# Attention's first score tiles ahead of the kernel's branch, V projected in two parts

## The chip, the cores and the metric

One core of a Trainium2 chip runs the kernel. The metric is the device time of one execution in microseconds, the median of several runs. Lower is better.

## The reference, cut to what matters

```python
x = x + xattn(layernorm(x), ctx_768, ...)      # x: 1 x 1024 x 128, ctx_768: 1 x 6404 x 96
x = x + ffn(layernorm(x), ...)                 # a main path and 2 of 8 experts, hidden size 512
...
q = (query @ Wq + bq)                          # 16 heads of 8
k = (key_value @ Wk + bk)
v = (key_value @ Wv + bv)
attn = clip(q k^T * 8 ** -0.5, -10000, 10000)
attn = softmax(attn)                           # 16 x 1024 x 6404
x = attn @ v
...
return x @ Wo + bo
```

The reference replaces attention by a mean where a NaN turns up and clips the scores. The kernel computes a bound of the scores at run time; if it holds, neither can occur and the softmax needs no maximum. That is the `safe` flag and the branch on it.

## The kernel before

**Stages.** The context (6404 rows of 96 numbers) is loaded, transposed on TensorE in 13 chunks of 512 rows into `ctxT` and projected to K^T, chunk by chunk (`ctx_transpose`, L941; `project_k`, L953). ScalarE evacuates both (`evac_ctxT`, L360; `evac_k`, L365). Meanwhile the queries are normalised (L571 to L595, scaled at L585), transposed, projected (L983) and evacuated (L496 to q, L498 to its absolute values).

**K and q through DRAM.** The score products run as sums over 32 rows, four heads side by side, each number split into a rounded part and a rest. VectorE makes the parts (`split_q` L616 and L618, `split_k` L626 and L627). SyncE stores them to DRAM (L396, L331) and loads them back in the layout of the products: `load_q` (L354, four loads of 128 KB a group of heads, each with a leading broadcast of 2), `load_k` (L341). K goes in ten segments of 5 tiles of 128 rows (the last with 4 rows more). The parts of a segment lie in one of two buffers, so that splitting segment s waits until segment s - 2 is stored:

```python
if s >= 2:
    dve.wait_ge(kparts_stored[s % 2], 16 * PARTS * (s // 2))
```

Each engine runs its instructions in the order in which they are written, and a wait holds up all behind it. In SyncE's queue q's loads stand ahead of K's first store.

**V and the bound.** Behind the K projections TensorE makes the bias rows (L992 to L994), V's 13 chunks (`project_v`, L964, evacuated by ScalarE, L373) and, between them, the bound (L1008, L1012, L1013). VectorE makes the flag (L669). Three chunks ahead of V's end the engines read it; ScalarE loads its Exp table there (L508). All that follows is written within the branch.

**The attention loop.** Eight passes (four groups of four heads, two halves of 512 queries each) go over the 51 K tiles. A score of one head and one K tile is a chunk of 128 x 512; three chunks are a score tile, in one of two PSUM buffers `ps`. For each of 500 tiles, TensorE computes the scores two tiles ahead (`score_tile`, L1077), ScalarE takes the exponential of all 128 x 1536 at once (L516) into one of four `probs` buffers, and TensorE multiplies with V (`values_step`, L1141, one step for each K tile once its four chunks are there; V's tail of 4 rows at L1127). The sums of a pass gather in one of the two banks `po`. The other bank is spare: `D_PLAN` names 27 steps of four chunks whose exponentials VectorE computes instead (L766 to L805), with the pass, the K tile, the tiles behind which its four scores are made, the heads' order, and the tile behind which its values are used. `SPARE` is the list of jobs in the spare bank, done strictly in turn: a job waits until VectorE has taken the one before it. At a pass's end the sums are transposed (L1099) and normalised. SyncE loads K for the next group behind its last use.

**The end.** Output projection, second normalisation and the feed-forward layers follow (L1017 to L1256). `region_ctx`, where the context stood, takes two experts' weights; `region_ctxT` held `ctxT` and then `probs`.

**POOL's work at the start:** constants, a row of ones in `ctxT` (a memset of 1 x 6432, L446), 12 small loads, the ones in V (`v9`, L460), more memsets.

Of the kernel before, what the change touches and what calls it, by code (L numbers as in the profile page):

```python
# [21 lines left out]
P = 128  # L22
# [31 lines left out]
V_ORDER = [0, KCH // 2] + [c for c in range(1, VCH) if c != KCH // 2]  # L54
NPR = 4
BO_BANK = 3 + (KCH - 3) % 3
FLAG_AHEAD = 3
BOUND_AT = 4
# [76 lines left out]
for gap in EPI_GAPS:  # L135
# [7 lines left out]

SPARE = sorted([(t, "score", GH * d + k) for d, (_, _, at, _, _) in enumerate(D_PLAN) for k, t in enumerate(at)]
               + [(NORM_AT[p], "tokens", p) for p in range(NP - 1)])
# [9 lines left out]
def tile_of_segment(p, s):  # L155
    return max(c for c, (n, _) in enumerate(CHUNKS)
               if STEPS[n][0] == p and (STEPS[n][1] < FULL and STEPS[n][1] // SEG_T == s)) // CPT
# [22 lines left out]
def build(nc, x, ctx, wq, bq, wk, bk, wv, bv, wo, bo, alpha, w_gate, b_gate, w1m, b1m, w2m, b2m,  # L180
# [4 lines left out]
    with ExitStack() as stack:  # L185
# [27 lines left out]
        pre = region_ctx[:, 2 * TOPK * HID:2 * TOPK * HID + CB * BANK].rearrange("p (c n) -> p c n", c=CB)  # L213
# [4 lines left out]
        ctxT = region_ctxT[0:CK + 1, 0:NK]  # L218
        tailT = sb("tailT", [CK + 1, P])
# [56 lines left out]
        probs = region_ctxT[:, 0:NPR * CPT * BANK].rearrange("p (b n) -> p b n", b=NPR)  # L276
# [25 lines left out]
        bounds_ready, bound_psum, gcol_ready, grow_psum, flag_ready = (sem(n) for n in ("bounds_ready", "bound_psum", "gcol_ready", "grow_psum", "flag_ready"))  # L302
# [8 lines left out]
        rows_psum, attention_done = sem("rows_psum"), sem("attention_done")  # L311
# [56 lines left out]
        def evac_v(act, nth):  # L368

            c = V_ORDER[nth]  # L370
            n = min(4, FULL + 1 - 4 * c)
            act.wait_ge(v_psum, nth + 1)
            act.activation(v9[:, 4 * c:4 * c + n, :, 0:D], po[nth % 2][:, 0:n * P].rearrange("p (t h d) -> p t h d", h=H, d=D),  # L373
                           ACT.Copy).then_inc(v_done, 1)


        def load_expert(engine, e):

# [6 lines left out]
        def _(sp):  # L385
# [17 lines left out]
            with sp.If(safe != 0):  # L403
                for s in range(1, NSEG):
                    store_k(sp, s)
                    if s >= 2:
                        load_k(sp, 0, s - 1)
# [886 lines left out]
```

## Time and profile before

| | |
|---|---|
| median of 3 runs | 794.51 us (794.29 to 796.16) |
| the profiled execution | 795.02 us |
| its span, first to last instruction | 793.2 us |
| TensorE busy | 728.6 us (92%) |
| ScalarE busy | 724.9 us (91%), of them 678.4 us in 500 exponentials |
| VectorE busy | 548.1 us (69%) |
| DMA engines' mean rate | 37 GB/s |

The durations below come from the profiled execution, whose time is 1.8 us over its span. PE is TensorE, PEld its weight loads, DVE VectorE, ACT ScalarE, POOL GpSimd, SPq the queue of SyncE. A product of f32 is two MATMUL instructions with a weight load each. Consecutive instructions of an engine overlap, so that what one costs is the distance from start to start. "[0.85 <-PE ps L1077]" says that the engine stood idle 0.85 us and what released it.

### The profile page before, as it was taken

What the parts mean: (1) busy time and instruction counts of PE and PEld (TensorE: products, weight loads), DVE (VectorE), ACT (ScalarE), POOL (GpSimd) and SP (SyncE); (2) the same over time, 40 slices, a digit from 0 to 9 for tenths busy, and PEclk for the clock granted to TensorE, in tenths of its full rate; (3) what the DMA queues carried; (4) which work ended last, traced back from release to release, by engine and by line L of the source; (5) the groups of instructions that cost most, each with busy time, mean ns of one, the idle gap of its engine ahead of it and who ended that gap; (6) DMA issues with size and microseconds to landing.
All of it is one profiled execution on the core that took longest, in us unless ns stands there. A gap on an engine that the chain in (4) does not pass through costs nothing.

```text
span 793.2 us, 13140 instructions
## 1 busy us (share of the span) xinstructions
PE 728.6 (92%) x5406; PEld 215.9 (27%) x5406; DVE 548.1 (69%) x760; ACT 724.9 (91%) x587; POOL 20.6 (3%) x36
## 2 busy tenths in 40 slices
PE   4988889999999999999899999999999989999898
PEld 2642222222222222222222222222222222222457
DVE  5634298789878978898788897897689882140220
ACT  3769999999999999999999999999999999999451
POOL 8000000000000000000000000000000000000000
PEclk9989999999999999999999999999999999999999
DMA  5258210011110000111100000111100000000010
GB/s 190 106 153 285 69 46 1 18 34 35 51 34 1 1 1 1 34 51 34 37 15 1 1 1 19 34 34 50 34 1 2 1 1 1 1 1 1 4 54 27
DMA packets 15324, 29.05 MB, mean 37 GB/s; under 512 B 2438, under 2 KB 5884, under 8 KB 15260
## 3 DMA queue, kind: packets, MB, share of 16 engines
q1 hardware_dynamic: 13562, 26.86, 11.0%
q8 instruction: 45, 0.74, 0.4%
q10 hardware_dynamic: 1218, 0.64, 0.3%
q0 software_dynamic: 480, 0.66, 0.3%
q14 instruction: 19, 0.16, 0.1%
HBM read 20.02 MB, written 8.13 MB: 35 GB/s over the span
## 4 chain that ended last, share of the span: by engine, by line
PE 53%; ACT 23%; issue 18%; DVE 3%; DMA 1%; POOLq 0%; SPq 0%; POOL 0%; ACTq 0%
PE po L1141 27%; ACT region_ctxT L516 22%; PE ps L1077 15%; PE ps L1222 2%; PE po L1232 1%; PE po L964 1%; PE ps L953 1%; DMA region_ctx<-in_ctx 1%; PE po L1127 1%; PE ps L941 1%; DVE xn L585 1%; PE po L1056 1%; DMA region_ctx<-in_w1e 0%; PE ps L1232 0%; PE ps L1072 0%
## 5 line engine op out<-in xcount | busy, mean ns | idle before, releaser
L516 ACT ACTIVATE region_ctxT<-ps 128x1536 f32<-128x1536 f32 x500 | 678.4, 1543 | 7.8 <-PE ps L1077 7.5
L1141 PE MATMUL po<-region_ctxT,v 128*9 128x512 f32 x2984 | 391.6, 597 | 0.5 <-ACT region_ctxT L516 0.5
L1077 PE MATMUL ps<-qst,region_k 32*128 32x512 f32 x1492 | 253.7, 495 | 42.3 <-ACT region_ctxT L516 41.5
L1077 PEld LDWEIGHTS ps<-qst,region_k 32*128 32x128 f32 x1492 | 97.2, 182 | 416.8 <-ACT region_ctxT L516 397.3
L766 DVE TENSOR_SCALAR region_kT<-po 128x512 f32<-128x512 f32 x108 | 74.1, 686 | 85.2 <-PE po L1077 85.2
L769 DVE SCALAR_TENSOR_TENSOR region_kT<-region_kT,po 128x512 f32<-128x512 f32 x108 | 73.4, 680 | 0.3
L1141 PEld LDWEIGHTS po<-region_ctxT,v 128*9 128x9 f32 x2984 | 44.3, 88 | 92.9 <-issue 89.4
L805 DVE SCALAR_TENSOR_TENSOR dres<-region_kT,dres 128x1024 f32<-128x1024 f32 x54 | 66.1, 1225 | 1.7
L802 DVE SCALAR_TENSOR_TENSOR dres<-region_kT,dres 128x1024 f32<-128x1024 f32 x54 | 65.8, 1218 | 0.1
L794 DVE SCALAR_TENSOR_TENSOR dres<-region_kT 128x1024 f32<-128x1024 f32 x54 | 65.7, 1218 | 0.0
L796 DVE SCALAR_TENSOR_TENSOR region_kT<-region_kT 128x1024 f32<-128x1024 f32 x54 | 65.7, 1217 | 0.0
L799 DVE SCALAR_TENSOR_TENSOR dres<-dres,region_kT 128x1024 f32<-128x1024 f32 x54 | 65.6, 1214 | 0.0
L1077 PE MATMUL po<-qst,region_k 32*128 32x512 f32 x108 | 52.1, 483 | 0.0
L785 DVE TENSOR_SCALAR region_kT<-region_kT 128x1024 uint32<-128x1024 uint32 x54 | 36.9, 683 | 0.0
L1141 PE MATMUL po<-dres,vd 128*9 128x512 f32 x216 | 28.2, 595 | 0.0
L748 DVE COPY region_kT<-po 128x512 f32<-128x512 f32 x8 | 5.5, 686 | 32.0 <-PE po L1127 32.0
L473 POOL TENSOR_TENSOR rstd<-rstd,powers 128x4 f32<-128x4 f32 x2 | 2.1, 1026 | 727.6 <-DVE rstd L580 727.6
L1077 PEld LDWEIGHTS po<-qst,region_k 32*128 32x128 f32 x108 | 19.6, 181 | 0.5 <-DVE region_kT L769 0.4
L703 DVE TENSOR_SCALAR region_ctx<-po,b1T 128x512 f32<-128x512 f32 x4 | 3.0, 751 | 19.2 <-PE po L1056 19.2
L360 ACT ACTIVATE region_ctxT<-ps 96x512 f32<-96x512 f32 (+1 forms) x13 | 7.5, 576 | 9.2 <-PE ps L941 9.2
L626 DVE CAST kparts<-region_kT 128x640 fp32r<-128x640 f32 (+1 forms) x10 | 4.9, 493 | 15.5 <-DMA k_dram<-kparts 14.5
L941 PE MATMUL ps<-ident,region_ctx 128*96 128x128 f32 x50 | 8.8, 309 | 7.2 <-DMA region_ctx<-in_ctx 7.2
(195 smaller groups left out, 304.3 us busy)
## 6 DMA issues: line engine op xcount, KB each, us to landing
region_k<-k_dram SPq DMA_DIRECT2D x40, 320.0 KB, 3.3
k_dram<-kparts SPq DMA_DIRECT2D x18, 320.0 KB, 4.3
qst<-q_dram SPq DMA_DIRECT2D x16, 128.0 KB
region_ctx<-in_ctx SPq DMA_DIRECT2D x2, 624.0 KB, 9.3
q_dram<-region_k SPq DMA_DIRECT2D x2, 512.0 KB, 2.7
k_dram<-kparts SPq DMA_DIRECT2D x2, 322.0 KB, 5.3
region_ctx<-in_ctx SPq DMA_DIRECT2D x1, 576.0 KB, 7.4
xres<-in_x SPq DMA_DIRECT2D x1, 512.0 KB, 4.4
```

The costliest lines, as they stand in the source:

```text
L516: act.activation(probs[:, t % NPR, :], ps[t % NSB][:, :], ACT.Exp, scale=ESCALE).then_inc(exp_ready, 1)
L766: d_count(("u", c), v.tensor_scalar(du[:, i % 2, part], src, MAGIC, None, ALU.add))
L769: v.scalar_tensor_tensor(df[:, i % 2, part], du[:, i % 2, part], MAGIC, src, ALU.subtract, ALU.subtract).then_inc(spare_taken, 1)
L785: d_count(("e", i), v.tensor_scalar(u.bitcast(U32), u.bitcast(U32), 23, None, ALU.logical_shift_left))
L794: d_count(("q1", i), v.scalar_tensor_tensor(res, f, A1, f, ALU.add, ALU.mult))
L796: d_count(("q2", i), v.scalar_tensor_tensor(q, f, A2, f, ALU.add, ALU.mult))
L799: d_count(("p1", i), v.scalar_tensor_tensor(res, res, B1, u, ALU.add, ALU.mult))
L802: d_count(("p2", i), v.scalar_tensor_tensor(res, q, B2, res, ALU.add, ALU.mult))
L805: v.scalar_tensor_tensor(res, f, R0, res, ALU.subtract, ALU.mult).then_inc(d_ready, 1)
L941: last = tr(dst[:, at:at + P], ctx_sb[:, t, :], ident[:, :])
L1077: return mm(dst, kst[r, kt * P:(kt + 1) * P], qst[r, g, queries], start=True, stop=True)
L1141: last = mm(dst[QUAD * j:QUAD * j + V9, :], w, src, start=first, stop=last_one, skip_group_check=True)
```

## The change

- **Order at the start.** `Sqrt`'s table load goes to ScalarE's beginning; the root comes behind the first chunk. K chunks run one earlier against the context's chunks. GpSimd's row of ones and the ones in V wait for the scaled queries.
- **V's chunks 0 to 4** are projected behind K's chunks 7 to 11 and taken by VectorE (`take_v`, L646 of the changed kernel) instead of ScalarE. Chunks 5 to 12 become spare jobs at tiles 5, 8, ... 26 of the first pass. So do the bound (tiles 3 and 6), its sum (9) and the bias rows (12).
- **Splits.** VectorE splits K's segments 0 to 3 behind its range reductions of chunks 2, 4, 7 and 9, segments 4 to 9 behind the spare jobs.
- **Ahead of the branch** stand now the Exp table load, the first 14 tiles, all K stores, the first group's K loads and all q loads.
- **Buffers.** `probs` move from `region_ctxT`, where ctxT is still read, to an own buffer and `region_ctx`; the absolute values of q are made by VectorE from q, and the bound's scale with them.
- **`D_PLAN`** keeps 27 steps, the first at tile 37 instead of 26, three instead of two in the last pass.

```diff
+NPRE = 14
+VPRE = 5
+V_AT = {c: 3 * c - 10 for c in range(VPRE, VCH)}
+BOUND_TILES, GSUM_TILE, ROWS_TILE = (3, 6), 9, 12
...
-    (0, 49, (26, 28, 31, 33), (3, 1, 2, 0), 48),
+    (0, 49, (37, 39, 42, 44), (0, 2, 3, 1), 56),
...
+    (7, 47, (479, 481, 485, 488), (3, 1, 0, 2), 499),
...
+SPLIT_BEHIND = {SPARE.index((V_AT[c], "v", c)): s for c, s in zip(range(VPRE, VCH), range(4, NSEG))}
...
+        probs_own = sb("probs_own", [P, CPT * BANK])
...
+            return probs_own[:, :] if n == 0 else region_ctx[:, (n - 1) * CPT * BANK:n * CPT * BANK]
...
             load_q(sp, 0)
-            store_k(sp, 0)
-            load_k(sp, 0, 0)
+            for s in range(NSEG):
+                store_k(sp, s)
+                if s != 1:
+                    load_k(sp, 0, max(s - 1, 0))
+            load_k(sp, 0, NSEG - 1)
+            load_k_tail(sp)
+            for g in range(1, NG):
+                load_q(sp, g)
             sp.wait_ge(flag_ready, 1)
...
+            pool.wait_ge(xn_ready, QT)
+            pool.memset(region_ctxT[CK:CK + 1, :], 1.0).then_inc(pads_ready, 1)
+            pool.wait_ge(pads_ready, 3)
+            pool.memset(v9[:, :, :, D:V9], 1.0).then_inc(vones_ready, 1)
...
+            act.activation(scratch[:, :], ones[0:1, 0:1], ACT.Exp).then_inc(table_step, 1)
...
+            exponentials(range(NPRE))
+            act.wait_ge(flag_ready, 1)
+            safe = act.value_load(flag[0:1, 0:1], min_val=0, max_val=1)
+            with act.If(safe != 0):
+
+                exponentials(range(NPRE, NT))
...
             for c in range(KCH - 1):
-                if c == 1:
+                if c == 3:
                     split_q()
+                    link(v.scalar_tensor_tensor(q_abs, qT[:, :], -1.0, qT[:, :], ALU.mult, ALU.max))
                 range_k(c)
-                if c == 4:
-                    split_k(0, link)
+                if c in (2, 4, 7, 9):
+                    split_k((2, 4, 7, 9).index(c), link)
+                if c >= KCH - 1 - VPRE:
+                    dve.wait_ge(v_psum, c - (KCH - 1 - VPRE) + 1)
+                    take_v(c - (KCH - 1 - VPRE), po[(c - (KCH - 1 - VPRE)) % 2]).then_inc(v_done, 1)
...
+                n = c - (KCH - 1 - VPRE)
+                if 0 <= n < VPRE:
+                    if n == 0:
+                        pe.wait_ge(q_ready, NHALF)
+                    if n >= 2:
+                        pe.wait_ge(v_done, n - 1)
+                    project_v(n, po[n % 2]).then_inc(v_psum, 1)
...
+                if kind == "v":
+                    last = project_v(i, po[1])
...
+            score_tile(0)
+            pe.wait_ge(k_ready, KCH)
+            score_tile(1)
...
+            score_tiles(range(NPRE))
+            pe.wait_ge(flag_ready, 1)
+            safe = pe.value_load(flag[0:1, 0:1], min_val=0, max_val=1)
+            with pe.If(safe != 0):
+                score_tiles(range(NPRE, NT))
```

The order of instructions, first on TensorE about the end of the K projections and the first scores. Before (L941 transposes, L953 K, L964 V, L1077 scores):

```order
L953 MATMUL ps<-region_ctxT,wk_sb 128x512 [waits k_ready,ctxT_ready] x2
L953 MATMUL ps<-region_ctxT,wk_sb 128x260 [waits k_ready,ctxT_ready]
L992 MATMUL ps<-bsum,ones 128x128 [waits k_ready,ffn_in]
L993 MATMUL ps<-mix,ones 128x1
L994 MATMUL ps<-ident,b1rows 128x36
L964 MATMUL po<-wv_sb,region_ctxT 128x128 [waits q_abs_ready,pads_ready,wv_in]
L964 MATMUL po<-wv_sb,region_ctxT 128x128 x7
L964 MATMUL po<-wv_sb,region_ctxT 128x128 [waits v_done]
```

Now (L983 transposes, L995 K, L1006 V, L1101 scores):

```order
L1006 MATMUL po<-wv_sb,region_ctxT 128x128 [waits v_done]
L1006 MATMUL po<-wv_sb,region_ctxT 128x128 x3
L983 MATMUL ps<-ident,region_ctx 96x128 [waits ctx_in4,ctxT_ready]
L983 MATMUL ps<-ident,region_ctx 96x128 [waits ctx_in4] x3
L995 MATMUL ps<-region_ctxT,wk_sb 128x512 [waits k_ready,ctxT_ready]
L1006 MATMUL po<-wv_sb,region_ctxT 128x128 [waits v_done]
L1006 MATMUL po<-wv_sb,region_ctxT 128x128 x3
L983 MATMUL ps<-ident,region_ctx 96x128 [waits ctx_in4,ctxT_ready]
L983 MATMUL ps<-ident,region_ctx 96x128 [waits ctx_in4]
L987 MATMUL ps<-ident,ctx_tail 96x4 [waits tail_in]
L995 MATMUL ps<-region_ctxT,wk_sb 128x512 [waits k_ready,ctxT_ready]
L1006 MATMUL po<-wv_sb,region_ctxT 128x128 [waits v_done]
```

V chunks whose place in PSUM is awaited (v_done) now stand ahead of the last K chunks, and the first scores stand right behind K.

On VectorE over the same stretch. Before (L611 range of K, L640 the tail of ctxT), nothing waits for a store between the first split and the last range:

```order
L626 CAST kparts<-region_kT 128x640
L627 TENSOR_TENSOR kparts<-region_kT,kparts 128x640 [waits dve_step]
L611 TENSOR_REDUCE kmax<-region_kT 128x1 [waits k_ready] x7
L640 COPY tailT<-region_ctxT 97x4 [waits pads_ready,ctxT_ready]
L640 COPY tailT<-region_ctxT 97x4 x3
L611 TENSOR_REDUCE kmax<-region_kT 128x1 [waits k_ready]
```

Now (L625 range of K, L640 and L641 the split, L646 V's evacuation):

```order
L625 TENSOR_REDUCE kmax<-region_kT 128x1 [waits k_ready] x3
L640 CAST kparts<-region_kT 128x640 [waits kparts_stored0]
L641 TENSOR_TENSOR kparts<-region_kT,kparts 128x640 [waits dve_step]
L646 COPY v<-po 128x64x8 [waits v_psum]
L625 TENSOR_REDUCE kmax<-region_kT 128x1 [waits k_ready]
L646 COPY v<-po 128x64x8 [waits v_psum]
L625 TENSOR_REDUCE kmax<-region_kT 128x1 [waits k_ready]
L640 CAST kparts<-region_kT 128x640 [waits kparts_stored1]
L641 TENSOR_TENSOR kparts<-region_kT,kparts 128x640 [waits dve_step]
L646 COPY v<-po 128x64x8 [waits v_psum]
```

Splits of segments 2 and 3, which wait for stores, stand ahead of V's evacuations.

At the end of TensorE's loop, now (L1186 and L1172 are `values_step`, L1223 the last pass's sums turned):

```order
L1186 MATMUL po<-region_ctx,v 9x512 [waits exp_ready]
L1186 MATMUL po<-region_ctx,v 9x512 x3
L1172 MATMUL po<-region_ctx,vtail 9x512 x4
L1186 MATMUL po<-dres,vd 9x512 [waits d_ready]
L1186 MATMUL po<-dres,vd 9x512 x3
L1223 MATMUL ps<-ident,region_kT 128x128 [waits o_taken]
```

The last step of all is now one whose exponentials VectorE made.

## Rows read from the trace of the kernel before

**Rows 1.** ScalarE in order of time: start, duration, work, count, idle before and releaser

```profile
47.84 1.28 ACT L508 ACT_TABLE_LOAD   x1 [0.15 <-issue]
49.13 0.20 ACT L508 ACTIVATE scratch<-ones 1x1 f32<-1x1 f32 x1
...
51.92 5.48 ACT L516 ACTIVATE region_ctxT<-ps 128x1536 f32<-128x1536 f32 x4 [0.60 <-PE ps L1077]
58.26 1.45 ACT L516 ACTIVATE region_ctxT<-ps 128x1536 f32<-128x1536 f32 x1 [0.85 <-PE ps L1077]
60.32 2.87 ACT L516 ACTIVATE region_ctxT<-ps 128x1536 f32<-128x1536 f32 x2 [0.62 <-PE ps L1077]
```

**Rows 2.** The same view, ScalarE near the end

```profile
699.55 37.98 ACT L516 ACTIVATE region_ctxT<-ps 128x1536 f32<-128x1536 f32 x28
```

**Rows 3.** The same view, TensorE within the second pass

```profile
110.78 1.04 PE L1141 MATMUL po<-region_ctxT,v 128*9 128x512 f32 x8
111.76 0.50 PE L1077 MATMUL ps<-qst,region_k 32*128 32x512 f32 x3
112.19 1.05 PE L1141 MATMUL po<-region_ctxT,v 128*9 128x512 f32 x8
```

**Rows 4.** The same view, TensorE ahead of the first scores

```profile
27.77 0.60 PE L941 MATMUL ps<-ident,region_ctx 128*96 128x128 f32 x4
...
29.07 0.60 PE L941 MATMUL ps<-ident,region_ctx 128*96 128x128 f32 x4
...
34.47 0.48 PE L992 MATMUL ps<-bsum,ones 1*128 1x128 f32 x2
...
35.18 4.85 PE L964 MATMUL po<-wv_sb,region_ctxT 97*128 97x128 f32 x40
39.96 1.90 PE L1008 MATMUL ps<-xn,bounds 128*32 128x512 f32 x4
```

**Rows 5.** SyncE's queue in order of time; last, a stretch with clock, DMA share, GB/s

```profile
24.52 1.58 SPq L396 DMA_DIRECT2D q_dram<-region_k  x2
28.51 2.67 SPq L354 DMA_DIRECT2D qst<-q_dram  x4
31.22 1.25 SPq L331 DMA_DIRECT2D k_dram<-kparts  x2
43.83 0.58 SPq L341 DMA_DIRECT2D region_k<-k_dram  x1
48.95 2.70 SPq L331 DMA_DIRECT2D k_dram<-kparts  x4
...
36.00:44.00 8.00, 8.00 (x59) 6.40 (x58) 3.55 (x17) 3.70 (x7) 0.00 (x0) 1.00 0.11 45
```

**Rows 6.** VectorE in order of time

```profile
11.51 0.20 DVE L592 RECIPROCAL rstd<-rstd 128x8 f32<-128x8 f32 x1 [3.16 <-ACT rstd L486]
...
12.39 5.24 DVE L585 TENSOR_SCALAR xn<-xres,mv,rstd 128x128 f32<-128x128 f32 x8
...
17.62 1.27 DVE L605 COPY xnT<-po 128x512 f32<-128x512 f32 x2
...
24.53 1.23 DVE L618 TENSOR_TENSOR region_k<-qT,region_k 128x1024 fp32r<-128x1024 f32 x1
...
53.47 0.49 DVE L626 CAST kparts<-region_kT 128x640 fp32r<-128x640 f32 x1 [3.28 <-DMA k_dram<-kparts]
54.00 0.82 DVE L627 TENSOR_TENSOR kparts<-region_kT,kparts 128x640 fp32r<-128x640 f32 x1
```

**Rows 7.** VectorE's scalings (line view: ns min/median/max), GpSimd in order of time

```profile
L585 DVE TENSOR_SCALAR xn<-xres,mv,rstd x16: 327/342/2098, 12.4 to 750.1; 128x128 f32<-128x128 f32 x16
...
14.94 1.62 POOL L460 MEMSET v<- 128x816 f32 x1
```

**Rows 8.** Stretches: busy PE, PEld, DVE, ACT, POOL, then granted clock, DMA share, GB/s

```profile
54.00:56.00 2.00, 1.36 (x10) 0.44 (x11) 0.82 (x1) 2.00 (x3) 0.00 (x0) 0.50 0.76 224
...
60.00:62.00 2.00, 1.77 (x17) 0.42 (x14) 0.79 (x1) 1.68 (x2) 0.00 (x0) 1.00 0.98 311
```

More of the change, by code:

```diff
@@ L497, in _, with exponentials @@
                                accum_out=ksum[:, KCH + n:KCH + n + 1]).then_inc(q_ready, 1)
[L498 to L501 removed]
+            for c in range(4, KCH):
+                if c + 1 < KCH:
+                    evac_ctxT(act, c + 1)
                 evac_k(act, c)
[L503 to L512 removed]
+            act.wait_ge(table_step, 1)
+            act.activation(scratch[:, :], ones[0:1, 0:1], ACT.Exp).then_inc(table_step, 1)
+            def exponentials(tiles):
+                for t in tiles:
                     act.wait_ge(scores_ready, t + 1)
@@ L671, in _ @@
+            for n in range(JOBS_PRE):
+                take_job(n, link)
             halves = [range(n * QT // 2, (n + 1) * QT // 2) for n in range(NHALF)]
@@ new lines, in _, with scores @@
+            seen = set()
+            def scores(dst, p, kt, j):
+                g, half = PASSES[p]
+                queries = slice(half * BANK, (half + 1) * BANK)
+                if ("q", g) not in seen:
+                    seen.add(("q", g))
+                    pe.wait_ge(qst_in[g], 16 * GH)
+                if kt == FULL:
+                    if "tail" not in seen:
+                        seen.add("tail")
+                        pe.wait_ge(ktail_ready, GH)
+                    return mm(dst, ktail[:, g, :], qst[:, g, queries], start=True, stop=True)
+                if (g, kt // SEG_T) not in seen:
+                    seen.add((g, kt // SEG_T))
+                    pe.wait_ge(kst_in[kt // SEG_T], 16 * (g + 1))
+                r = slice(QUAD * j, QUAD * (j + 1))
+                return mm(dst, kst[r, kt * P:(kt + 1) * P], qst[r, g, queries], start=True, stop=True)
@@ new lines, in values_step @@
+            def values_step(n):
+                t, kind, i = VALUES[n]
+                p = VALUES_PASS[n]
+                kt = STEPS[i][1] if kind == 0 else D_PLAN[i][1]
+                first, last_one = n == VALUES_OF_PASS[p][0], n == VALUES_OF_PASS[p][-1]
+                dst = po[pv_bank(p)]
+                if first and p == 0:
+                    pe.wait_ge(vones_ready, 1)
+                    pe.wait_ge(v_done, VPRE)
+                if p == 0 and kt % 4 == 0 and kt // 4 in V_AT:
+                    pe.wait_ge(spare_taken, SPARE_OF["v", kt // 4] + 1)
+                if first and p >= 1:
+                    used = sum(at <= t for at, _, _ in SPARE)
+                    if used:
+                        pe.wait_ge(spare_taken, used)
+                    if p >= 2:
+                        pe.wait_ge(o_taken, p - 1)
+                if kt == FULL:
+                    c = CHUNKS.index((i, None))
+                    tile, m = divmod(c, CPT)
+                    if p == 0:
+                        pe.wait_ge(vtail_ready, GH)
+                    for j in range(GH):
+                        r = slice(QUAD * j, QUAD * (j + 1))
+                        last = mm(dst[QUAD * j:QUAD * j + V9, :], vtail[r, PASSES[p][0], QUAD * j:QUAD * j + V9],
+                                  probs_of(tile)[r, m * BANK:(m + 1) * BANK],
+                                  start=first, stop=last_one, skip_group_check=True)
+                else:
+                    if kind == 1:
+                        pe.wait_ge(d_ready, 2 * (i + 1))
+                    for j in range(GH):
+                        if kind == 0:
+                            tile, m = divmod(CHUNKS.index((i, j)), CPT)
+                            src = probs_of(tile)[:, m * BANK:(m + 1) * BANK]
+                        else:
+                            k = D_PLAN[i][3].index(j)
+                            src = dres[:, i % 2, k * BANK:(k + 1) * BANK]
+                        w = v9[:, kt, GH * PASSES[p][0] + j, :] if kind == 0 else vd[:, i % 2, V9 * j:V9 * (j + 1)]
+                        last = mm(dst[QUAD * j:QUAD * j + V9, :], w, src,
+                                  start=first, stop=last_one, skip_group_check=True)
+                last.then_inc(pv_done, 1)
@@ L1150, in _, with score_tiles @@
+            score_tile(0)
+            pe.wait_ge(k_ready, KCH)
+            score_tile(1)
+            def score_tiles(tiles):
+                for t in tiles:
                     if t + NSB < NT:
@@ L1179, in _ @@
             with pe.Else():
+                pe.wait_ge(exp_ready, NPRE)
+                for n in range(JOBS_PRE, JOBS_V):
+                    spare_job(n)
                 with pe.Fori(0, H) as h:
```

329 lines of the change are left out of this document (131 added, 198 removed), and 45 rows, old and new, of the table D_PLAN.

## The prediction

> **What bounds the kernel now.** I read the page first, then ScalarE's and TensorE's order of time, then the queue. ScalarE does 500 exponentials of three score banks. The first begins at 51.92 us and the next three follow in one row of 5.48 us, so one costs (5.48 - 1.45) / 3 = 1.34 us [rows 1]; near the end 28 of them still take 37.98 us, (37.98 - 1.45) / 27 = 1.35 us, and the last ends at 699.55 + 37.98 = 737.53 us [rows 2]. So 670 of the 793 us are one unbroken row of exponentials, and a change can win only before its first, inside it where it breaks, or behind its last. TensorE is close behind: a score tile takes 0.43 us (111.76 to 112.19) and a values step 0.98 us (110.78 to 111.76) [rows 3]. Four tiles carry three values steps, 4 x 0.43 + 3 x 0.98 = 4.66 us against ScalarE's 5.36: **a slack of 0.18 us a tile**, and no more.
>
> Ahead of the first exponential stand the K chunks at 1.30 us each (transposes and projection, 27.77 to 29.07), then the 13 V chunks at 4.78 / 5 = 0.96 us (35.18 to 39.96) [rows 4]. The first exponential waits for the scores behind them [rows 1], no longer for the way of K through DRAM, whose first load was issued at 43.83 [rows 5].
>
> **The queue.** That first load waited. The q stores go out at 24.52, q's four loads from 28.51 to 31.18, K's first stores at 31.22; only at 43.83 is the store landed, and from 36 to 44 us the DMA engines are busy at a share of 0.11, some two of sixteen [rows 5]. So q's loads run on two engines and K's first store, which has a part on each engine, ends behind them: 43.83 - 25.76 = **18.1 us after VectorE has split q** (24.53 + 1.23) [rows 6]. Before, nothing was held by it. After, something is.
>
> **The change, part by part.** I count from the profiled execution's 795.02 us.
>
> *Queries earlier.* VectorE idled 3.16 us for the square root, behind a chunk's evacuation and a table load that now comes at the start; I leave 0.3 us of it. Its eight scalings then took 5.24 us [rows 6], with some at 2098 ns where the least is 327; eight at 0.3 us take 2.4 us, and the GpSimd work that ran beside them now waits for them [rows 7]. Normalised rows are thus complete near 12.0 instead of 17.6 us. TensorE reaches their transposes at about 13.0, then one K chunk (1.30) and two query products of four 0.43 us passes (1.7), ScalarE 0.7: q at about 18.1, VectorE's split in 1.9 to 2.3 us, end 20.4 against 25.8, **5.4 us earlier**. K's first store then lands at 43.8 - 5.4 = 38.4. Against it: VectorE's casts now meet GpSimd's memset of the ones in V (1.62 us) and its DMA issues. Rows show two scalings of about 2.1 us in such company, a loss of 1.8 each [rows 7]; none is the low bound, two the high, 38.4 to 42.1, and I take 39.5.
> The Trainium skill's page "SBUF — State Buffer", section "SBUF: two separate sides", says that VectorE in a two-port mode and GpSimd lock each other out for the whole instruction. By that rule every cast that meets a GpSimd memset pays in full, and the landing would be at the late bound; the trace shows stalls of that kind for some of the scalings and not for their neighbours.
>
> *A wait that was harmless now stands on the path.* VectorE splits K segment 2 at chunk 7, and that waits until segment 0 is stored, 39.5 us. Behind it on VectorE stand all evacuations of V's first five chunks; behind those on TensorE, V's third chunk and with it K's chunks 10 to 12 and all scores. TensorE would be through chunk 9 near 27 us (17.3 + 6 x 1.30 + 2 x 0.96). From the landing on, as 0: VectorE splits 1.35 (53.47 to 54.82) and copies V 0.64 [rows 6], 2.0; TensorE V 3.0, K 4.3, V 5.2, K 6.5; V's fifth chunk waits for the third's evacuation, which stands behind the split of segment 3, whose store is issued at 0.6 and lands 4.5 us later, as 48.95 did to 53.47 [rows 5, 6]: 5.1 + 1.35 + 0.64 = 7.1. V 8.1, K's last 260 columns 8.5, evacuation 9.1, Exp table load 1.28 and the dummy activation [rows 1]: **10.6 us** at full clock. But TensorE has idled 12 us. Before, after a stretch with gaps, it ran at half clock (0.50 from 54 to 56, that is 1.2 GHz) and was at 1.00 from 60 on [rows 8]. With every product at twice its time from 2.0 on, the sum is 15.8. No row tells when it comes back here, somewhere within this chain most likely, so I take a little under the middle, 12.8. First exponential: 39.5 + 12.8 = 52.3 against 51.92, **+0.4 us**, between 49.0 and 57.9.
> The table load that now stands ahead of the first exponential costs 1.29 us by the row, since the activation begins at 49.13 behind the load of 47.84. The Trainium skill's page "ScalarE: Activation LUTs", section "What ACT_TABLE_LOAD costs", adds a drain, 2.66 us in all; by that the first exponential would come 1.4 us later and the sum below would be 6.8 us.
>
> *Warm TensorE.* The half clock fell into the first tiles before; exponentials 5 and 6 waited 0.85 and 0.62 us and their starts (58.26 and 60.32 against 51.92 + 5 x 1.34 = 58.6 for the sixth) lag by 1.7 us [rows 1]. After, the slow stretch is spent before the first exponential: **-1.7 us** (0 if it isn't).
>
> *V in the first pass.* Eight chunks, the last with three tiles, 7.4 us; the two bound products 1.90, bias rows 0.71 (34.47 to 35.18) [rows 4]; together 10.0 us in tiles 3 to 26. ScalarE's 24 tiles leave 24 x 0.18 = 4.3 us of slack. What is over goes onto the path, since TensorE issues scores in order behind these jobs and two score tiles are all that is ahead: **+5.7 us**. No wait for VectorE is added: a V copy and a split take 2.0 us against three tiles' 4.0. If weight loads hid half of V's cost, it is 2.0. The branch is read by each sequencer ahead of its engine and costs nothing while exponentials run; if it shows, 1 us.
>
> *The end.* The tile count stays 500, the VectorE steps 27. Of them three now fall in pass 7, and the last one's values stand behind the last exponential and V's tail step, as one more values step ahead of the last sums: **+1.0 us** [rows 3]. Other moved steps cost TensorE the same, elsewhere; I give the pass ends 0, within 1.5 us either way. probs in another region, queries' absolute values on VectorE (idle then), and x's bound chain cost nothing: VectorE's cover is its idle time in the first pass.
>
> Sum: 0.4 - 1.7 + 5.7 + 1.0 = **+5.4 us**, 800.4 for the profiled execution, which stands 0.5 over the median; for the median **800.0 us**.
>
> **Rivals.**
> *A, the store lands early.* If K's first store doesn't queue behind q's loads, VectorE is never held, TensorE is through near 35 us, and q's landing sets the first exponential, 39.5. Then -12.4 - 1.7 + 5.7 + 1.0 = -7.4, 787 us: faster. It decides if the store lands before about 28 us. For it, typical stores take some 4.5 us; against it, the same code was in the same order in the queue and took 12. Chance 0.10.
> *B, TensorE hides V.* Weight loads and gaps take V's products in and the first pass stays on ScalarE's 1.34: 0.4 - 1.7 + 0.7 + 1.0 = +0.4, 795 us, no change. For it, the page books matmul time of which part is pipeline; against, V's chunks stood back to back at 0.96. Chance 0.2.
> *C, cold start.* Half clock through the whole chain and on into the first tiles, both casts stalled: 57.9, +6.0 + 0 + 5.7 + 1.0 = +12.7, 807 us. Chance 0.12.
> *D, it does not do what it says:* score tiles move ahead of the branch but not earlier in time. That is my forecast, chance 0.58.
>
> **How the numbers follow.** A measurement can tell 0.3%, 2.4 us, from no change. Forecast D alone spans 794 to 804 (landing 38.4 to 41, chain 10.6 to 15, V 4 to 6.5). Range 792 to 806: it leaves out A's and most of C's, some 0.2. Faster: A and the low end of B, 0.14. Same, 792.1 to 796.9: most of B and D's low end, 0.21. Slower: 0.65.
>
> **What would show it.** VectorE's CAST of kparts at chunk 7 waits some 10 us or more for k_dram<-kparts, to 38 to 42 us; TensorE idle from 27 to about 41, half clock behind it; first exponential at 49 to 58, with the table load just ahead. Between the first exponential and the 30th, 29 x 1.34 + about 5.7 = 44.6 us. Last exponential near 742, a dres values step behind the tail step. It is wrong if the CAST doesn't wait, if the first exponential stands under 45 us, or if the first 30 tiles take under 41 us.

## The result, and the profile after

The changed kernel takes **803.41 us** (median of 4 runs, 802.85 to 806.88) against 795.18 us (4 runs, 794.29 to 796.16): ratio 1.0116, 95% interval 1.0087 to 1.0144. It is slower, by 1.2%. The forecast was 800.0 us within 792 to 806.

| | before | after |
|---|---|---|
| profiled execution, its span | 795.02, 793.2 us | 802.85, 801.1 us |
| first exponential | 51.92 | 53.42 |
| exponential 1 to 31 (start to start) | 41.77 | 49.41 |
| 31 to 51 | 26.80 | 26.61 |
| 51 to 500 | 615.59 | 613.77 |
| last exponential's start to the end | 57.1 | 57.9 |

The last five rows differ by +1.5, +7.6, -0.2, -1.8 and +0.8 us, together the 7.9 us between the spans. Nearly all of the loss lies in the first 30 tiles.

VectorE in order of time (start, duration, work, count, idle before and releaser), against [rows 6]:

```profile
9.39 2.14 DVE L598 TENSOR_SCALAR xn<-xres,mv,rstd 128x128 f32<-128x128 f32 x8
...
16.39 1.87 DVE L625 TENSOR_REDUCE kmax<-region_kT 128x1 f32<-128x512 f32 x3
18.18 0.92 DVE L640 CAST kparts<-region_kT 128x640 fp32r<-128x640 f32 x1
...
19.87 0.69 DVE L630 CAST region_k<-qT 128x1024 fp32r<-128x1024 f32 x1
20.59 1.22 DVE L632 TENSOR_TENSOR region_k<-qT,region_k 128x1024 fp32r<-128x1024 f32 x1
...
41.54 0.49 DVE L640 CAST kparts<-region_kT 128x640 fp32r<-128x640 f32 x1 [14.23 <-DMA k_dram<-kparts]
...
47.56 0.49 DVE L640 CAST kparts<-region_kT 128x640 fp32r<-128x640 f32 x1 [2.29 <-DMA k_dram<-kparts]
```

The scalings now take 2.14 us instead of 5.24 and q is split by 20.59 + 1.22 = 21.81, 4.0 us earlier than before. Then comes the wait that the forecast rested on: VectorE stands 14.23 us before K's segment 2, until segment 0 is stored.

The chain of waits over the same stretch, in order of time (start, duration, what); it follows that wait back to q's stores and forward to the first exponential:

```profile
21.85 4.92 DMA q_dram<-region_k
...
30.16 11.36 DMA k_dram<-kparts
...
41.54 0.50 DVE kparts L640
...
43.55 2.07 PE po L1006 x8
...
47.84 0.89 PE po L1006 x8
...
52.01 1.28 ACT L514
...
53.31 0.20 ACT scratch L514
```

From the landing at 41.54 to the exponential at 53.42 is 11.9 us. V's third chunk takes 2.07 us in this view and the fourth 0.89: the third ran at half clock.

SyncE's queue, against [rows 5]:

```profile
20.59 1.58 SPq L401 DMA_DIRECT2D q_dram<-region_k  x2
26.79 2.67 SPq L368 DMA_DIRECT2D qst<-q_dram  x4
29.50 1.25 SPq L345 DMA_DIRECT2D k_dram<-kparts  x2
41.53 0.58 SPq L355 DMA_DIRECT2D region_k<-k_dram  x1
```

Stretches (busy PE, PEld, DVE, ACT, POOL, then granted clock, DMA share, GB/s), against [rows 8]:

```profile
34.00:40.00 6.00, 0.00 (x0) 0.00 (x0) 0.00 (x0) 0.00 (x0) 0.00 (x0) 0.50 0.13 52
44.00:46.00 2.00, 2.00 (x11) 1.97 (x11) 1.27 (x3) 0.00 (x0) 0.00 (x0) 0.50 0.97 329
50.00:52.00 2.00, 1.91 (x14) 1.26 (x12) 1.80 (x4) 1.17 (x4) 0.00 (x0) 1.00 0.88 250
...
58.00:60.00 2.00, 2.00 (x15) 0.42 (x11) 0.00 (x0) 1.12 (x2) 0.00 (x0) 0.50 0.00 0
62.00:64.00 2.00, 2.00 (x16) 0.48 (x8) 0.68 (x1) 1.25 (x1) 0.00 (x0) 1.00 0.00 0
```

From 34 to 40 us no engine works, and the DMA engines are busy at a share of 0.13, as much as two of sixteen. The granted clock is half behind that gap, full at 50, and **half again** over the first tiles. ScalarE shows what that costs, against [rows 1]:

```profile
54.75 4.08 ACT L522 ACTIVATE region_ctx<-ps 128x1536 f32<-128x1536 f32 x3
59.71 1.45 ACT L522 ACTIVATE probs_own<-ps 128x1536 f32<-128x1536 f32 x1 [0.88 <-PE ps L1101]
61.80 1.45 ACT L522 ACTIVATE region_ctx<-ps 128x1536 f32<-128x1536 f32 x1 [0.64 <-PE ps L1101]
64.07 2.79 ACT L522 ACTIVATE region_ctx<-ps 128x1536 f32<-128x1536 f32 x2 [0.81 <-PE ps L1101]
```

TensorE at a V chunk in the first pass and at the end, against [rows 3, 4]:

```profile
70.35 1.16 PE L1006 MATMUL po<-wv_sb,region_ctxT 97*128 97x128 f32 x8
71.44 0.50 PE L1101 MATMUL ps<-qst,region_k 32*128 32x512 f32 x3
...
746.66 1.04 PE L1186 MATMUL po<-dres,vd 128*9 128x512 f32 x8
```

A V chunk costs 71.44 - 70.35 = 1.09 us, not the 0.96 it took when five stood back to back [rows 4]. At the end the dres step stands last, 0.98 us behind the tail step's start at 745.68.

### The profile page after: what moved, and what is told of

It is laid out like the page before. It is cut to its first block, busy times and chain, and to the rows that moved or that the text cites. A ratio compares the mean times of both kernels' runs of the same rounds, so it can differ in the third digit from the quotient of the medians.

```text
span 801.1 us, 13262 instructions
## 1 busy us (share of the span) xinstructions
PE 731.0 (91%) x5406; PEld 218.6 (27%) x5406; DVE 553.9 (69%) x776; ACT 717.9 (90%) x572; POOL 21.0 (3%) x36
## 4 chain that ended last, share of the span: by engine, by line
PE 56%; ACT 20%; issue 17%; DMA 3%; DVE 3%; SPq 1%; POOLq 0%; POOL 0%; ACTq 0%
PE po L1186 30%; PE ps L1101 16%; ACT region_ctx L522 14%; ACT probs_own L522 5%; PE ps L1278 2%; PE po L1006 2%; DMA k_dram<-kparts 1%; PE po L1288 1%; DMA region_ctx<-in_ctx 1%; PE po L1172 1%; PE ps L995 1%; DMA q_dram<-region_k 1%; PE po L1101 1%; PE po L1081 1%; DMA region_ctx<-in_w1e 0%
## 5 line engine op out<-in xcount | busy, mean ns | idle before, releaser
L522 ACT ACTIVATE region_ctx<-ps 128x1536 f32<-128x1536 f32 x375 | 528.6, 1511 | 8.2 <-PE ps L1101 7.9
L1186 PE MATMUL po<-region_ctx,v 128*9 128x512 f32 x2238 | 390.8, 596 | 0.5 <-ACT region_ctx L522 0.5
L1101 PE MATMUL ps<-qst,region_k 32*128 32x512 f32 x1492 | 252.6, 495 | 38.4 <-ACT region_ctx L522 25.9
L1101 PEld LDWEIGHTS ps<-qst,region_k 32*128 32x128 f32 x1492 | 96.6, 182 | 410.8 <-ACT region_ctx L522 289.2
L1186 PE MATMUL po<-probs_own,v 128*9 128x512 f32 x746 | 192.9, 598 | 0.0
L522 ACT ACTIVATE probs_own<-ps 128x1536 f32<-128x1536 f32 x125 | 188.9, 1511 | 3.0 <-PE ps L1101 2.6
L1186 PEld LDWEIGHTS po<-region_ctx,v 128*9 128x9 f32 x2238 | 42.2, 88 | 70.0 <-issue 66.3
L1101 PE MATMUL po<-qst,region_k 32*128 32x512 f32 x108 | 51.4, 476 | 0.0
L1006 PE MATMUL po<-wv_sb,region_ctxT 97*128 97x128 f32 x100 | 15.1, 296 | 15.7 <-DVE v L646 15.7
L1186 PE MATMUL po<-dres,vd 128*9 128x512 f32 x216 | 28.2, 595 | 0.0
L1186 PEld LDWEIGHTS po<-probs_own,v 128*9 128x9 f32 x746 | 19.6, 88 | 22.9 <-issue 22.6
L646 DVE COPY v<-po 128x512 f32<-128x512 f32 (+1 forms) x13 | 8.8, 677 | 21.7 <-PE po L1006 21.7
```

The costliest lines, as they stand in the source:

```text
L522: act.activation(probs_of(t), ps[t % NSB][:, :], ACT.Exp, scale=ESCALE).then_inc(exp_ready, 1)
L1006: last = mm(dst[:, (t % 4) * P:(t % 4 + 1) * P], lhsT, wv_sb[:, :], start=True, stop=True)
L1101: return mm(dst, kst[r, kt * P:(kt + 1) * P], qst[r, g, queries], start=True, stop=True)
L1186: last = mm(dst[QUAD * j:QUAD * j + V9, :], w, src, start=first, stop=last_one, skip_group_check=True)
```

## The experiments

Times are compared with runs of the kernel before on the same chip: 795.63 us for e1 to e4, 794.72 for e5 to e8, 795.09 for e9 to e11. "Changed kernel" is the one of this document's diff; each edit is against it unless it says otherwise. The ratios are to that kernel before, as recorded with their 95% intervals; they differ by up to some 0.2% from the quotients of the medians. A difference to the changed kernel is one between runs of different series, so the profiled executions carry the argument where it is small. The theory: VectorE's place behind K's first store holds the first exponential back, that store is held by q's loads on two DMA engines, and V's chunks in the first pass fall on the path.

### e1: the two waiting splits behind V

```diff
-                if c in (2, 4, 7, 9):
-                    split_k((2, 4, 7, 9).index(c), link)
+                if c in (2, 4):
+                    split_k((2, 4).index(c), link)
...
             link(v.tensor_reduce(kcol[:, 0:1], kmax[:, :], AX.X, ALU.max))
+            split_k(2, link)
+            split_k(3, link)
```

> The changed kernel with the splits of K's segments 2 and 3 moved on VectorE behind V's evacuations and the last range reduction. If VectorE's wait for segment 0's store holds V and with it TensorE, TensorE now ends its K and V products near 34 us instead of 51, the wait for the store (still to about 41.5 us) stands on no path but K's first load, and the first exponential comes at 41.5 + 0.6 + 3.3 + 0.5 = about 46 us instead of 53.4: 7 to 7.5 us less, near 796 us. If the start is bound by something else (the queries' landing, the table load), the first exponential stays over 51 us and the time at 803.

Measured: 796.31 us, ratio 1.0005 (0.9991 to 1.0019). VectorE in order of time:

```profile
41.38 0.49 DVE L640 CAST kparts<-region_kT 128x640 fp32r<-128x640 f32 x1 [5.87 <-DMA k_dram<-kparts]
```

TensorE, the last K projection and the first scores:

```profile
33.39 0.60 PE L997 MATMUL ps<-region_ctxT,wk_sb 96*128 96x260 f32 x2
44.93 1.22 PE L1103 MATMUL ps<-qst,region_k 32*128 32x512 f32 x6 [10.94 <-DMA region_k<-k_dram]
```

The store lands as late as ever (41.38), but only the splits wait for it. K and V are finished at 34, and the first exponential comes at 45.77, 0.84 us behind the scores' start and 7.7 us earlier; the first 30 tiles stay at 49.82. So the order on VectorE is worth about 7 us of the time. What stands on the path now is the store and the load behind it.

### e2: q's loads on all DMA engines

The four loads with a leading broadcast of 2 become eight without one.

```diff
-                sp.dma_start(qst[QUAD * j:QUAD * (j + 1), g, :].bitcast(F32),
-                             rows.unsqueeze(0).broadcast_to([PARTS, PARTS * D, NQ])).then_inc(qst_in[g], 16)
+                for a in range(PARTS):
+                    r = slice(QUAD * j + a * PARTS * D, QUAD * j + (a + 1) * PARTS * D)
+                    sp.dma_start(qst[r, g, :].bitcast(F32), rows).then_inc(qst_in[g], 16)
```

> The changed kernel with each of q's loads written as two loads of 16 rows without the leading broadcast of 2. If q's loads are slow because they run on two of sixteen DMA engines, K's first store lands behind eight issues (26.8 to 31.7 us) and some 4 us, at 35 to 36.5 instead of 41.5; VectorE's wait shortens by 5 to 6 us, the rest of the chain stays at some 12, and the time falls by 5 to 6 us, near 798. If the store is late for another reason (traffic of other loads), it lands within 1 us of 41.5 and nothing changes but the queue's longer issue.

Measured: 797.14 us, ratio 1.0026 (1.0008 to 1.0045); first exponential 46.86. SyncE's queue:

```profile
26.70 4.03 SPq L370 DMA_DIRECT2D qst<-q_dram  x8
30.77 1.27 SPq L345 DMA_DIRECT2D k_dram<-kparts  x2
34.90 0.57 SPq L355 DMA_DIRECT2D region_k<-k_dram  x1
```

Twice as many loads take 1.4 us longer to issue (4.03 against 2.67), and K's store behind them lands after 34.90 - 30.77 = 4.1 us instead of 12.0. VectorE's wait ends 6.6 us earlier and the first exponential comes 6.6 us earlier: the chain behind the landing stays 12.0 us. This confirms the queue half of the theory, in all of its size. The edit takes away the broadcast and doubles the number of loads, so that it alone does not tell these two apart.

### e5: the same in the kernel before

> The kernel before, with q's loads written without the leading broadcast of 2, as eight loads. If q's slow loads only matter where VectorE waits for the store behind them, the first K load is issued some 6 us earlier than 43.83 us and nothing else moves: the first exponential stays at 51.9, the time within 0.3% of the kernel before. If the start of the kernel before hung on them too, 4 us or more less.

Measured: 794.83 us, ratio 1.0003 (0.9993 to 1.0012). SyncE's load behind the store, and ScalarE's first exponentials:

```profile
36.55 0.58 SPq L341 DMA_DIRECT2D region_k<-k_dram  x1
```

```profile
51.92 5.48 ACT L517 ACTIVATE region_ctxT<-ps 128x1536 f32<-128x1536 f32 x4 [0.61 <-PE ps L1078]
```

Its store lands at 36.55, 7.3 us earlier than in [rows 5], and its first exponential starts at 51.92 as in [rows 1]. Before the change nothing was held by that store. So the change did not make the store slow; it put it on the path.

### e3 and e4: V's chunks in the first pass

e3 puts them at every fourth tile, e4 computes each of the eight twice.

```diff
-V_AT = {c: 3 * c - 10 for c in range(VPRE, VCH)}
+V_AT = {c: 4 * (c - VPRE) + 4 for c in range(VPRE, VCH)}
```

```diff
                 if kind == "v":
+                    project_v(i, po[1])
                     last = project_v(i, po[1])
```

> The changed kernel with V's chunks 5 to 12 as jobs at tiles 4, 8, ... 32 instead of 5, 8, ... 26. If the jobs cost what TensorE's work goes over ScalarE's time, eight more tiles of slack (0.18 us each) and chunks placed where no values step stands give back 1.5 to 2.5 us. If the cost is a wait for VectorE's taking of each job, the same waits remain and the time stays within 0.5 us.

> The changed kernel with each of V's eight chunks in the first pass computed twice into the same bank. If TensorE is the bound there, the second computation costs in full, 8 times 1.0 us, so 7.5 to 8.5 us more. If TensorE hides V in gaps, under 3 us more.

Measured: e3 801.89 us, ratio 1.0066 (1.0040 to 1.0092), first 50 tiles 75.03 us against 76.02. e4 812.46 us, ratio 1.0190 (1.0158 to 1.0222), first 50 tiles 83.54. TensorE in e4:

```profile
73.36 2.05 PE L1006 MATMUL po<-wv_sb,region_ctxT 97*128 97x128 f32 x16
75.34 0.50 PE L1101 MATMUL ps<-qst,region_k 32*128 32x512 f32 x3
```

The second copy of a chunk takes 1.98 - 1.09 = 0.89 us; 7.75 of them (the last chunk has three tiles of four) are 6.9, and the first 50 tiles grew by 7.5. All that TensorE is given there beyond what it has falls on the path, which excludes the rival that it hides V (0.7 us for all). The medians lie 9.1 us apart; the rest stands elsewhere in the profile: the first exponential comes at 54.93, 1.5 us later, and tiles 51 to 500 take 615.46 us, 1.7 more, with a granted clock of one half from 419.0 to 422.4. Spreading the chunks wins 1.0 us, short of the 1.5 to 2.5 expected: the jobs end at tile 32 instead of 26, and six more tiles, not eight, give their slack of 0.18 us, 1.1 us.

### e6: TensorE kept busy

17 dummy products of 512 columns stand where TensorE waits for VectorE, three more behind score tile 1. They go into banks that are overwritten.

```diff
+                    if n == 2:
+                        pe.wait_ge(ctxT_ready, 9)
+                        for _ in range(17):
+                            mm(bank(2, P, BANK), ones[:, :], xnT[:, 0:BANK], start=True, stop=True)
...
             score_tile(1)
+            pe.wait_ge(v_done, VPRE - 1)
+            for _ in range(3):
+                mm(po[1][:, :], ones[:, :], xnT[:, 0:BANK], start=True, stop=True)
```

> The changed kernel with products added whose results nobody reads: 17 of 512 columns into a free bank before TensorE's wait for V's third chunk (some 14.6 of the 15.7 us), and 3 behind the second score tile, where TensorE waits for the Exp table and the first exponential. If the half clock costs what I read, the granted clock stays full, the way from the store's landing to the first exponential falls from 11.9 to some 10.7 us, and the first tiles lose 1.5 us less: 2.5 to 3 us in all, near 800.5. If the losses there are VectorE's and the queue's alone, the time stays at 803.

Measured: 802.09 us (800.03 to 804.89), ratio 1.0107 (1.0083 to 1.0132). Stretches, columns as above:

```profile
44.00:46.00 2.00, 2.00 (x15) 1.52 (x14) 0.97 (x2) 0.86 (x2) 0.00 (x0) 1.00 1.01 353
58.00:60.00 2.00, 2.00 (x17) 0.51 (x13) 0.36 (x1) 2.00 (x2) 0.00 (x0) 1.00 0.00 0
```

ScalarE:

```profile
52.41 1.42 ACT L522 ACTIVATE probs_own<-ps 128x1536 f32<-128x1536 f32 x1
53.73 4.08 ACT L522 ACTIVATE region_ctx<-ps 128x1536 f32<-128x1536 f32 x3
57.73 1.42 ACT L522 ACTIVATE probs_own<-ps 128x1536 f32<-128x1536 f32 x1
```

In the profiled execution the granted clock is 1.00 throughout, and the stalls of the fifth and sixth exponentials are gone. From the landing (VectorE's CAST at 41.23) to the first exponential is 11.2 us instead of 11.9, and the first 30 tiles take 47.34 instead of 49.41. So half clock cost 0.7 us ahead of the first exponential and 2.1 in the tiles, by this one profile; the runs themselves scatter by more (the median is 1.3 lower, and the two ratios' intervals overlap), so the sum of 2.8 is shown by the trace alone. Nor did the clock stay full in every run: two of the four had a mean granted clock of 1.000 and took 800.03 and 800.63 us, the other two 0.996 with 803.55 and 804.89. It also isolates V: with no half clock, 30 tiles take 47.34 - 30 x 1.34 = **7.1 us** too long.

### e7: the Exp table load early

It stands right behind the square root instead of ahead of the first exponential.

```diff
             act.activation(rstd[:, 1, :], rstd[:, 0, :], ACT.Sqrt).then_inc(std_ready, 1)
+            act.wait_ge(table_step, 1)
+            act.wait_ge(const_ready, 3)
+            act.activation(scratch[:, :], ones[0:1, 0:1], ACT.Exp).then_inc(table_step, 1)
```

> The changed kernel with the load of the Exp table put right behind the square root at 8.5 us instead of behind K's last evacuation (no other function in between needs another table). By the trace's 1.28 and 0.2 us the first exponential comes 1.4 us earlier, 802; by the Trainium skill's figure with a drain it would be 2.7 us. TensorE idles 1.4 us less there, so the half clock may not return, worth 1 to 1.5 us more.

Measured: 805.65 us, ratio 1.0132 (1.0110 to 1.0154): slower, against the expectation. ScalarE:

```profile
8.80 1.28 ACT L498 ACT_TABLE_LOAD   x1
10.10 0.20 ACT L498 ACTIVATE scratch<-ones 1x1 f32<-1x1 f32 x1
...
55.23 0.19 ACT L379 ACTIVATION_READ_ACCUMULATOR region_kT<-ps 128x1 f32 x1
55.39 1.45 ACT L522 ACTIVATE probs_own<-ps 128x1536 f32<-128x1536 f32 x1
```

The CAST of segment 2 was released at 44.91. The chain from the landing fell from 11.9 to 55.39 - 44.91 = 10.5, by 1.4 us: the load and its dummy, and no more. The half clock came back all the same, from 57.7 to 64.5 us, against what was hoped. But the landing came 3.4 us later. At 8.80 the load holds up the context's evacuations, on which TensorE and then q depend: q's stores were issued 1.7 us later (22.27) and took 7.8 us instead of 6.2; why they took longer is not shown. The place of the load was cheaper where it was.

### e10: GpSimd's late loads behind q's stores

In the changed kernel ten loads of GpSimd (0.6 MB, issued from 18.60 to 24.77) run beside q's stores, which take 26.79 - 20.59 = 6.2 us to the first load, against 4.0 before.

```diff
+            pool.wait_ge(qparts_stored, 16 * PARTS)
             for dst, src in ((bsum[0:1, 0, :], bo), (wo_sb
```

> The changed kernel, with GpSimd's ten late loads behind q's stores. Theory (those loads hold q's stores up by 2.2 us on engines that both use): CAST of segment 2 released at 39.3 instead of 41.5, first exponential at 51.2, median 801.2. Rival (the stores take their time by themselves): CAST at 41.5, first exponential 53.4, median 803.4.

Measured: 805.34 us, ratio 1.0135 (1.0120 to 1.0150). SyncE's queue:

```profile
25.52 2.67 SPq L368 DMA_DIRECT2D qst<-q_dram  x4
28.24 1.31 SPq L345 DMA_DIRECT2D k_dram<-kparts  x2
42.47 0.58 SPq L355 DMA_DIRECT2D region_k<-k_dram  x1
```

The stores land after 4.8 us, 1.4 sooner, and K's store after 14.2, 2.2 later: the landing is at 42.47 and the first exponential at 54.69. Both accounts missed. The late loads do hold q's stores; moved, they are issued from 25.79 to 31.27, beside q's loads and K's store, and what was won is lost there.

### e11: K's first store ahead of q's

```diff
+            store_k(sp, 0)
             for b in range(PARTS):
                 sp.wait_ge(qparts_ready, b + 1)
...
+            load_k(sp, 0, 0)
             load_q(sp, 0)
-            for s in range(NSEG):
+            for s in range(1, NSEG):
```

> The changed kernel, with segment 0's K store ahead of q's stores in SyncE's queue and its load ahead of q's loads; q's loads stay on two engines. Theory (it is the place in the queue behind q's loads that holds VectorE): the CAST of segment 2 no longer waits, but segment 3's waits for segment 1's store, which now stands behind q's loads and lands near 43; only V's fourth copy and later work stand behind it, so first exponential at 47 to 49, median 797.5 to 799.5. Rival (one held store is as bad as the other, the chain behind it starts at its landing): first exponential at 53 or later, median 803 or more.

Measured: 801.32 us, ratio 1.0070 (1.0052 to 1.0088). VectorE:

```profile
27.28 0.48 DVE L642 CAST kparts<-region_kT 128x640 fp32r<-128x640 f32 x1
...
45.46 0.49 DVE L642 CAST kparts<-region_kT 128x640 fp32r<-128x640 f32 x1 [14.45 <-DMA k_dram<-kparts]
```

Segment 2 no longer waits; segment 3 does, 14.45 us, for the store that now stands behind q's loads. The held store is the expected one, but q's stores beside K's let the first load start only after 29.94 - 21.36 = 8.6 us instead of 6.2, so the landing is at 45.46 instead of 43, and the first exponential at 52.35, not at 47 to 49; the time lies between the two accounts' 797.5 to 799.5 and 803. Little is won by turning one store round while q's loads run on two engines.

### e8 and e9: a version that beats both

e8 takes e1, e2, e7, e10 and e11 together and projects V's chunks 0 to 6 ahead of the scores, the other six at every fifth tile. e9 is the same without e7.

```diff
-VPRE = 5
-V_AT = {c: 3 * c - 10 for c in range(VPRE, VCH)}
+VPRE = 7
+V_AT = {c: 5 * (c - VPRE) + 4 for c in range(VPRE, VCH)}
```

> All remedies together on the changed kernel: splits 2 and 3 behind V's evacuations, q's loads on all engines, K's first store ahead of q's stores and its first load ahead of q's loads, GpSimd's ten loads behind q's stores, the Exp table early, seven V chunks ahead instead of five, the other six as jobs every fifth tile. TensorE then works without a wait to about 35 us (eight steps of 1.30 and seven of 0.89 from 18.1), q lands near 33, the first exponential at 36 instead of 53.4, and the first pass loses 1 us instead of 9.4. If each remedy does what I say, 803.4 - 17 - 5 to 7 = 780 to 783; it is 785 or more if a wait that I don't see takes their place.

> The combined version with the Exp table load back where the change has it, right ahead of the first exponential. Theory (the table load itself costs 1.3 us wherever it stands; its early place holds up the context's evacuations and costs some 2 us of preparation, 3.5 seen alone): q is split about 2 us earlier, so q and K land about 2 us earlier, the table load takes 1.3 us back: first exponential 37 to 39 against 39.02, median 785.0 to 786.5. Rival (with nothing waiting for q any more the early place costs nothing): first exponential at 40.3, median 788.

Measured: e8 **786.73 us** (785.27 to 791.03), ratio to the kernel before **0.9912** (0.9889 to 0.9934), 16.7 us under the changed kernel. e9 788.04 us, ratio 0.9916 (0.9896 to 0.9936). ScalarE in e8:

```profile
38.86 0.19 ACT L380 ACTIVATION_READ_ACCUMULATOR region_kT<-ps 128x1 f32 x1
39.02 1.45 ACT L526 ACTIVATE probs_own<-ps 128x1536 f32<-128x1536 f32 x1
```

TensorE's first scores, which wait for nothing:

```profile
38.47 1.14 PE L1107 MATMUL ps<-qst,region_k 32*128 32x512 f32 x6
```

The first exponential starts at 39.02, right behind K's last evacuation; K's first load and q's loads had been issued from 28.68 to 34.07, and no wait for DRAM is left ahead of it. Against the changed kernel that is 14.4 us, and the first 50 tiles (73.86 instead of 76.02) give 2.2. With these waits gone the changed order wins 8.0 us over the kernel before; what of it the score tiles ahead of the branch bring by themselves was not run. The time missed the expected 780 to 783. The first exponential came 3 us later than the 36 expected: TensorE ended K at 38.5 instead of 35, q was split at 23.1 instead of 21.8, behind the early table load, and TensorE waited once more for VectorE, 1.13 us at 26.9. And the first 50 tiles still take 73.86 - 50 x 1.34 = 6.9 us too long, where 1 us was expected for the pass.

In e9 the table load (at 38.24) costs the start only 0.6 us (39.64), since the preparation runs 0.8 us earlier; but the first 30 tiles take 47.73 against 46.57, with half clock from 42 to 49 instead of from 44 to 47. The start came out late of the theory's 37 to 39 and early of the rival's 40.3, the time at the rival's 788. The intervals of e8 and e9 overlap, so which place of the table load is better here stays open.

## Why the prediction was right or wrong

The profiled execution was forecast at +5.4 us and came out at +7.8. The result lies in the range, on the side that had 0.65. In part that is luck: the first three terms below came out 4.7 us over their forecasts together, the last two 2.2 us under theirs.

| term | forecast | measured | how |
|---|---|---|---|
| first exponential | +0.4 | +1.5 | 53.42 - 51.92 |
| warm TensorE | -1.7 | +0.5 | half clock cost 2.1 (49.41 - 47.34 of e6) against 41.77 - 30 x 1.34 = 1.6 before |
| V in the first pass | +5.7 | +7.1 | 47.34 - 30 x 1.34, e6 |
| rest of the passes | 0 +- 1.5 | -2.0 | 26.61 - 26.80, 613.77 - 615.59 |
| the end | +1.0 | +0.8 | 57.9 - 57.1 |

**The mechanism was right.** The CAST waited 14.23 us for K's store, to 41.54 (forecast: over 10 us, to 38 to 42), TensorE stood from 27.8 to 43.55, and the first exponential at 53.42 lies within 49 to 58. e1 and e2 each remove one link, and the wait goes or shrinks as it should. Rival A (the store lands early) needed a landing before 28; only the combined versions are free of any wait for a store. Rival D, the forecast, describes what happened: the first exponential stayed where it was, 1.5 us later. Of rival C one part came true, half clock in the first tiles. The forecast's own sign for the 29 tiles from the first to the 30th exponential, 44.6 us, failed: they took 47.99, and the two steps on V and the clock below are what is missing (1.4 and 2.1).

**Queries 5.4 us earlier: 4.0.** q's last evacuation ended at about 19, not 18.1. And the step left out that segment 0's split stands ahead of q's on VectorE: 19.87 - 18.18 = 1.7 us, of which 0.9 came behind q's evacuation. The scalings were sized right (2.14 against 2.4).

**Casts against GpSimd.** One of the two stalled: 0.92 us instead of 0.48, its start at 18.18 within GpSimd's memset of 17.16 + 1.59. A loss of 0.4, against the 1.1 taken. The same CAST began within that memset in e1, e2, e3, e4 and e6 too: it took from 0.82 to 1.45 us and ended 0.35 us behind the memset each time, and in e7 to e11, where it began behind the memset, it took 0.48 to 0.50. The Trainium skill's "SBUF — State Buffer", section "SBUF: two separate sides", says that of a GpSimd instruction and one of VectorE in a two-port mode the one that starts first keeps the shared port for its whole length; these rows agree. So what is paid is the rest of the memset and not a fixed price. The later CAST at 24.18, beside GpSimd's DMA issues, took 0.48.

**From q's split to the landing: 18.1 taken, 19.7 measured** (41.53 - 21.81). q's stores took 2.2 us longer beside GpSimd's loads (e10 gives these 1.4 of it, and the rest stays open), the loads and K's store 0.6 less. The forecast moved q ahead on VectorE and did not ask what it would meet on the DMA engines. Together the landing came at 41.5 instead of 39.5.

**The chain behind it: 12.8 taken, 11.9 measured**, 11.2 at full clock (10.6 worked out). Half clock, until 47.4, fell on V's third chunk, on the transposes of the context's chunk 11 and on most of K's chunk 10, and part of it was hidden by segment 3's store: in e6, at full clock, TensorE waited 0.87 us behind that store for V's fifth chunk, here not at all. The table load cost 1.28 us and the activation came 1.30 behind its start, as in [rows 1]. The Trainium skill's "ScalarE: Activation LUTs", section "What ACT_TABLE_LOAD costs", has 2.66 us with a drain; without the load (e7) the chain fell by 1.4, so no drain shows here.

**Warm TensorE: this step failed.** It took for granted that a slow stretch is spent once, and forecast -1.7 us; measured is +0.5. The clock was full at 50 and half again from 54 to 61, and the same exponentials stalled as before. A half clock over the first tiles does not need a long wait ahead of them: the kernel before had it too (52.7 to 59.5 us), and so had e8 and e9.

**V in the first pass: mis-sized.** 1.09 us a chunk instead of 0.96 gives 7.75 x 0.13 = 1.0 of the 1.4 us that were missing. That it falls on the path in full, e4 shows. Rival B is out.

**The rest: -2.0, just outside 1.5.** ScalarE's exponentials grouped (count, busy, mean ns, idle before), before from 120 to 730 us and after from 128 to 737:

```profile
L516 ACT ACTIVATE region_ctxT<-ps 128x1536 f32<-128x1536 f32 x446 | 605.9, 1532 | 5.8 <-PE ps L1077 5.5 <-PE ps L1072 0.2
```

```profile
L522 ACT ACTIVATE region_ctx<-ps 128x1536 f32<-128x1536 f32 x335 | 472.2, 1513 | 2.7 <-PE ps L1101 2.7
L522 ACT ACTIVATE probs_own<-ps 128x1536 f32<-128x1536 f32 x112 | 169.6, 1514 | 1.1 <-PE ps L1101 0.7 <-PE ps L1096 0.3
```

ScalarE waits for scores 3.8 us instead of 5.8. All runs of the changed kernel but e4 repeat it, with 613.6 to 613.9 us for tiles 51 to 500 against 615.6. The rearranged `D_PLAN` is what I put it down to; `probs` lie elsewhere too, and neither was tried alone.

## What to carry to other kernels

A wait that is written where nothing stands behind it is free; put work behind it on the same engine, and the slowest transfer of the queue sets the time. Before work is moved ahead of a barrier, list for each of its inputs which queue brings it and what stands in front there. And work given to an engine with 0.18 us of slack a tile is on the path as soon as that slack is used up: of some 11 us given to TensorE in the first pass, 7.1 showed. Count that slack before work is moved there.

## What the runs showed of the hardware

**Loads with a leading broadcast of 2 kept no more than two DMA engines busy.** The share is 0.13 from 34 to 40 us, two of sixteen, and K's store issued behind them landed after 12.0 us; with eight loads without the broadcast it took 4.1 (e2, e5), and the share was 0.74 from 31 to 34 us (e2). The Trainium skill's "DMA: Bandwidth & Descriptors", section "Rules for kernel authors", says that a leading broadcast of c copies confines a DMA to c engines at most; the traces agree.

**The half clock comes back.** In the changed kernel TensorE stood idle for 15.73 us, was granted 1.2 GHz from 30.3 to 47.4, 2.4 GHz to 54.2, and 1.2 GHz again to 61.0, though it was busy in all of 58 to 60. Ahead of the second drop it had stood idle for 2.34 us, from 52.6 on. With dummy products in the gaps the profiled execution of e6 kept 2.4 GHz. e6 filled both gaps at once, but e8 and e9 have no long one: TensorE waits there for 1.14 us at most between 15 us and its first scores, and the clock falls over the first tiles all the same, from 43.6 to 47.0 in e8, behind gaps of 0.91 and 0.93 us, and from 41.8 to 48.7 in e9, behind one of 2.34. So the drop over the first tiles needs no long idle stretch ahead of the scores; whether the short gaps alone make it was not run.

**Loads of one queue slow another's stores.** GpSimd's 0.6 MB cost 1.4 us beside q's stores; moved behind them, K's store took 2.2 us longer, 14.2 instead of 12.0 (e10).

**A CAST of VectorE that begins within a GpSimd memset ends just behind it.** In six runs it ended 0.35 us behind the memset's end, whatever its start, and took 0.82 to 1.45 us instead of 0.48.
